# A mixture-of-experts stage with weights stationary, in blocks of 240 gathered tokens instead of tiles of 128

## The reference

```python
x = x + xattn(layernorm(x), ctx, ctx, ...)
x = x + ffn(layernorm(x), ...)
...
probs = softmax(xf @ router_w.T); topk_p, topk_i = top_k(probs, 2)
topk_p = topk_p / topk_p.sum(-1)
for e in range(8):
    mask = (topk_i == e).any(-1); w_tok = (topk_p * (topk_i == e)).sum(-1)
    mean_w = w_tok.sum() / mask.sum()
    h = silu(xf @ gate_w[e].T) * (xf @ up_w[e].T)          # 256 -> 1024
    out += mask[:, None] * (h @ down_w[e].T) * mean_w      # 1024 -> 256
```

## Time and profile before

| | |
|---|---|
| device time, median of 3 runs | 531.59 us (530.47 to 532.20) |
| profiled execution: span from first to last instruction | 528.9 us |
| instructions | 10721 |
| PE matmul busy | 476.4 us (90%) |
| PE weight loads busy | 375.3 us (71%) |
| DVE busy | 321.5 us (61%) |
| ACT busy | 265.6 us (50%) |
| POOL busy | 186.4 us (35%) |
| mean granted TensorE clock | 0.954 of full speed |
| DMA traffic | 46.26 MB, mean 87 GB/s |

### The profile page before, as it was taken

The page is one execution under the profiler, slowest core; times in us unless marked ns, Lnnn a source line. Parts: engine busy times, 40 slices in busy tenths (PEclk is TensorE's granted clock), DMA queues, the critical chain, the costliest instruction groups (busy, mean ns, idle before and its releaser), DMA issues. The chain is left out here.

```text
span 528.9 us, 10721 instructions
## 1 busy us (share of the span) xinstructions
PE 476.4 (90%) x2879; PEld 375.3 (71%) x2880; DVE 321.5 (61%) x827; ACT 265.6 (50%) x878; POOL 186.4 (35%) x211
## 2 busy tenths in 40 slices
PE   2999999999999983199999999999999999999980
PEld 2656666665666542078888888888888888888870
DVE  3476988989998656345665456655655555553430
ACT  1287777677777870044544445544444444532320
POOL 5201327355372434712332323323333232232232
PEclk9699999999999995579999999999999999999996
DMA  7166102112020171371531634415317212112110
GB/s 210 33 184 241 32 12 54 32 34 63 7 58 14 50 286 47 96 274 32 168 117 35 215 83 139 147 32 196 101 20 256 42 20 32 27 21 39 20 20 10
DMA packets 21738, 46.26 MB, mean 87 GB/s; under 512 B 5032, under 2 KB 18600, under 8 KB 20684
## 3 DMA queue, kind: packets, MB, share of 16 engines
q10 hardware_dynamic: 1982, 23.29, 11.6%
q1 hardware_dynamic: 12974, 14.34, 9.3%
q0 software_dynamic: 6752, 8.29, 9.2%
HBM read 34.21 MB, written 10.04 MB: 84 GB/s over the span
## 5 line engine op out<-in xcount | busy, mean ns | idle before, releaser
L752 ACT ACTIVATE probs<-b_s,negmax 100x100 f32<-100x100 f32 x256 | 85.6, 358 | 25.2 <-DVE negmax L1005 21.8
L615 PE MATMUL b_s<-w_hi,x_hi 128*128 128x512 f32 x180 | 77.1, 428 | 1.1 <-issue 1.1
L617 PE MATMUL b_s<-w_hi,x_lo 128*128 128x512 f32 x180 | 72.3, 402 | 0.0
L616 PE MATMUL b_s<-w_lo,x_hi 128*128 128x512 f32 x180 | 72.2, 401 | 0.0
L640 PE MATMUL b_pv<-w_hi,h_hi 128*128 128x256 f32 x240 | 69.8, 291 | 1.4 <-DVE h_lo L1102 1.4
L640 PE MATMUL b_pv<-w_hi,h_lo 128*128 128x256 f32 x240 | 67.4, 281 | 0.0
L640 PE MATMUL b_pv<-w_lo,h_hi 128*128 128x256 f32 x240 | 67.3, 280 | 0.0
L1245 POOL TENSOR_SCALAR y_sb<-y_raw,mean 128x256 f32<-128x256 f32 x30 | 32.8, 1093 | 75.9 <-DVE y_raw L1109 75.7
L1250 POOL DMA_INDIRECT out<-y_sb,idnow x30 | 49.1, 1638 | 25.6 <-issue 23.0
L780 ACT CAST h_hi<-b_small 128x512 fp32r<-128x512 f32 x30 | 17.6, 587 | 80.7 <-PE b_small L631 80.7
L1116 DVE TENSOR_TENSOR w_lo<-w_raw,w_hi x84 | 57.3, 682 | 0.0
(11 more groups left out here) (142 smaller groups left out, 1004.1 us busy)
## 6 DMA issues: line engine op xcount, KB each, us to landing
w_raw<-in_ffw ACTq DMA_DIRECT2D x7, 3072.0 KB, 10.1
xin<-slots SPq DMA_DIRECT2D x30, 128.5 KB
w_raw<-in_ffw SPq DMA_DIRECT2D x1, 3072.0 KB, 10.8
kblk<-krot SPq DMA_DIRECT2D x128, 12.5 KB, 1.8
out<-x_all SPq DMA_DIRECT2D x8, 200.0 KB
ctx_all<-in_ctxT SPq DMA_DIRECT2D x1, 1200.0 KB, 6.1
x_all<-in_x SPq DMA_DIRECT2D x1, 1200.0 KB
cst<-in_consts SPq DMA_DIRECT2D x1, 539.0 KB, 7.5
```

The costliest lines, as they stand in the source:

```text
L615: pe.matmul(o, lh, rh, start=(k == 0), stop=False)
L616: pe.matmul(o, lh, rl, start=False, stop=False)
L617: m = pe.matmul(o, ll, rh, start=False, stop=(k == n - 1))
L752: m = nc.scalar.activation(probs[:, N % 3, h, :], b_s[N % 3][0:S, h * S:(h + 1) * S], ACT.Exp, bias=negmax[:, N % 4, h:h + 1], accum_out=p ...
```

## The change

The expert stage is rewritten. A block is 240 gathered tokens, in two groups of 120 rows (`GRP`, `ROWS`, `TILE`). In gate and up the weights are now the stationary operand and the block's 240 tokens the moving one, so the result comes out as features x tokens, for one chunk `f` of 128 hidden features at a time (eight chunks, `FC`). It is already in the form that the down projection needs, and `hidden_transpose` is gone. The down projection runs per chunk and group: 3 matmuls with 120 stationary and 256 moving columns, for 2 groups.

ACT makes `h_hi` of a chunk from `h_sb` in SBUF (which DVE's `gated` has written), not from a transposed PSUM bank. The weights of the next expert are split in six pieces of 1024 columns (`WC`, `WCH`), one after each of the first six chunks of the expert's first block. There is one `w_raw` buffer in place of two; each piece is loaded again (`reload`, on ACT's queue) once its low part is made. The scale by the mean weight is done by ACT's `take_output`, straight from PSUM; POOL only copies row numbers and issues two indirect DMAs per block. The tails are gone: SP fills `slots` with padding rows by DRAM to DRAM DMAs during the attention stage (`fill_pads`, 8 for each of the first seven pairs), and POOL's scatter waits for those that cover its rows. SP reads the loop's two values ahead of the wait for the scatters. ACT's loop over experts is written out. The plan word loses its third field.

```diff
-TILE = 128
+GRP = 2
+ROWS = 120
+TILE = GRP * ROWS
...
-WC = 512
-CH = WT // WC
-WCH = THIRDS * CH
+WC = WT // 2
+WCH = 6
...
@@ sync
+            def fill_pads(j):
+                for e in range(E):
+                    base = e * REGION + j * TILE
+                    sp.dma_start(slots[base:base + TILE, :].rearrange("(p g) w -> p (g w)", g=GRP),
+                                 padrows.rearrange("(p g) w -> p (g w)", g=GRP)).then_inc(s_pre[j], 16)
...
                     key_blocks(i + 1)
+                if i < MAXT:
+                    fill_pads(i)
...
-                sp.wait_ge(s_tails[e], 16)
...
@@ tensor
+            def hidden(par, f):
+                cols = slice(f * P, (f + 1) * P)
+                for which, banks, done in ((0, b_gate, s_gate), (1, b_up, s_up)):
+                    wh, wl = wpart(w_hi[par])[which], wpart(w_lo[par])[which]
+                    o = banks[f % 2][:, 0:TILE]
+                    for c in range(DC):
+                        pe.matmul(o, wh[:, c, cols], x_hi[:, c, :], start=(c == 0), stop=False)
+                        pe.matmul(o, wh[:, c, cols], x_lo[:, c, :], start=False, stop=False)
+                        m = pe.matmul(o, wl[:, c, cols], x_hi[:, c, :], start=False, stop=(c == DC - 1))
+                    m.then_inc(done, 1)
+            def project_down(par, t, f):
+                pe.wait_ge(s_hlo, FC * t + f + 1)
+                if f == 0:
+                    pe.wait_ge(s_y, t + 1)
...
+                for g in range(GRP):
+                    o = b_y[g // 2][0:ROWS, g % 2 * D:(g % 2 + 1) * D]
+                    for k, (left, right) in enumerate(((h_hi, wh), (h_hi, wl), (h_lo, wh))):
+                        m = pe.matmul(o, left[:, f, g * ROWS:(g + 1) * ROWS], right[:, f, :], ...)
+            def step(t, par, next_par, next_split, following):
+                for f in range(1, FC):
+                    if f >= 2:
+                        pe.wait_ge(s_h, FC * t + f - 1)
+                    if f == FC - 1:
...
+                            pe.wait_ge(s_xlo, t + 1)
+                            tile_transpose(t + 1)
+                    hidden(par, f)
+                    if f >= 2:
+                        project_down(par, t, f - 2)
+                project_down(par, t, FC - 2)
...
                     pe.wait_ge(s_wlo, next_split)
                     pe.wait_ge(s_xlo, t + 2)
                     hidden(next_par, 0)
+                project_down(par, t, FC - 1)
@@ scalar
+            def hidden_high(t, f):
+                a.wait_ge(s_h, FC * t + f + 1)
+                nc.scalar.copy(h_hi[:, f, :], h_sb[:, f % 2, :]).then_inc(s_hhi, 1)
+            def weights_high(e, par, k):
+                a.wait_ge(s_raw[k], 16 * (e + 1))
+                cols = slice(k * WC, (k + 1) * WC)
+                nc.scalar.copy(w_hi[1 - par][:, cols], w_raw[:, cols]).then_inc(s_whi, 1)
+            def reload(e, k):
+                a.wait_ge(s_wlo, WCH * (e + 1) + k + 1)
+                a.dma_start(w_raw[:, k * WC:(k + 1) * WC],
+                            ffw[e + 2][:, k * WC:(k + 1) * WC]).then_inc(s_raw[k], 16)
+            def take_output(t, e):
+                a.wait_ge(s_down, t + 1)
+                a.wait_ge(s_idnow, t + 1)
...
+                    m = nc.scalar.activation(y_sb[:, 2 * n:2 * n + 2, :].rearrange("p g d -> p (g d)"),
+                                             b_y[n][0:ROWS, :], ACT.Copy, scale=meanw[0:ROWS, e:e + 1])
+            def step(t, e, par, split, again, final=False):
+                for f in range(FC):
+                    if f:
+                        if f == FC - 1 and not final:
+                            a.wait_ge(s_up, FC * (t + 1))
+                            x_high(t + 1)
+                        silu(t, f)
+                    hidden_high(t, f)
+                    if split and f < WCH:
+                        weights_high(e, par, f)
+                    if split and again and 1 <= f <= WCH:
+                        reload(e, f - 1)
                 if not final:
                     silu(t + 1, 0)
+                take_output(t, e)
@@ vector
+            def gated(t, f):
+                v.wait_ge(s_up, FC * t + f + 1)
+                v.wait_ge(s_act, FC * t + f + 1)
+                V.tensor_tensor(h_sb[:, f % 2, :], b_up[f % 2][:, 0:TILE], act[:, f % 2, :], ALU.mult).then_inc(s_h, 1)
+            def hidden_low(t, f):
+                v.wait_ge(s_hhi, FC * t + f + 1)
+                V.tensor_tensor(h_lo[:, f, :], h_sb[:, f % 2, :], h_hi[:, f, :], ALU.subtract).then_inc(s_hlo, 1)
+            def weights_low(e, par, k):
+                v.wait_ge(s_whi, WCH * e + k + 1)
+                cols = slice(k * WC, (k + 1) * WC)
+                V.tensor_tensor(w_lo[1 - par][:, cols], w_raw[:, cols], w_hi[1 - par][:, cols],
+                                ALU.subtract).then_inc(s_wlo, 1)
+            def step(t, e, par, split, final=False):
+                for f in range(FC):
+                    if f:
+                        if f == FC - 1 and not final:
+                            x_low(t + 1)
+                        gated(t, f)
+                    hidden_low(t, f)
+                    if split and f < WCH:
+                        weights_low(e, par, f)
+                    if f == FC - 2 and not final:
+                        v.wait_ge(s_idnow, t + 1)
+                        take_ids(t + 1)
                 if not final:
                     gated(t + 1, 0)
+            def expert(e, par):
+                lo, hi, end, _ = tiles_of(v, e)
+                step(lo, e, par, True)
+                with v.If(end - lo), v.Fori(lo + 1, hi) as t:
+                    step(t, e, par, False)
@@ gpsimd
-            for e in range(E):
-                G.indirect_dma_start(slots, bass.IndirectOffsetOnAxis(taili[:, e:e + 1], 0),
-                                     tailrow[:, :], None).then_inc(s_tails[e], 16)
...
+                for n in range(GRP):
+                    G.indirect_dma_start(out, bass.IndirectOffsetOnAxis(idnow[:, n:n + 1], 0), y_sb[:, n, :], None,
...
+                                         compute_op=ALU.add).then_inc(s_add, 16)
```

More of the change, by code:

```diff
@@ L642, in project_down @@
-                m.then_inc(s_down, 1)
-            def step(t, par, split_down, next_par, next_split, following):
-                hidden_transpose(t, 0)
-                hidden(par, 1)
-                with ExitStack() as s:
-                    if following is not None:
-                        s.enter_context(pe.If(following))
-                    tile_transpose(t + 1)
-                pe.wait_ge(s_wlo, split_down)
-                pe.wait_ge(s_y, t + 1)
-                project_down(par, t, 0)
-                hidden_transpose(t, 1)
+                        m = pe.matmul(o, left[:, f, g * ROWS:(g + 1) * ROWS], right[:, f, :],
+                                      start=(f == 0 and k == 0 and g % 2 == 0), stop=(f == FC - 1 and k == 2),
+                                      skip_group_check=True)
@@ L783, in weights_high @@
-            def weights_high(par, third, chunk):
-                if third is None:
-                    return
-                col = third * WT + chunk * WC
-                nc.scalar.copy(w_hi[1 - par][:, bass.ds(col, WC)], w_raw[par][:, bass.ds(col, WC)]).then_inc(s_whi, 1)
-            def step(t, third, par, final=False):
-                hidden_high(t, 0)
-                weights_high(par, third, 0)
-                silu(t, 1)
-                weights_high(par, third, 1)
-                if not final:
-                    x_high(t + 1)
-                weights_high(par, third, 2)
-                hidden_high(t, 1)
-                weights_high(par, third, 3)
+                for c in range(DC):
+                    m = nc.scalar.copy(x_hi[:, c, :], b_xt[c][:, 0:TILE])
@@ L1086, in x_low, with take_ids @@
                 v.wait_ge(s_xhi, t + 1)
-                V.tensor_tensor(x_lo[:, :, :].rearrange("p c t -> p (c t)"), b_xt[:, 0:DC * TILE],
-                                x_hi[:, :, :].rearrange("p c t -> p (c t)"), ALU.subtract).then_inc(s_xlo, 1)
-            def take_ids(t, column):
+                for c in range(DC):
+                    ins = V.tensor_tensor(x_lo[:, c, :], b_xt[c][:, 0:TILE], x_hi[:, c, :], ALU.subtract)
+                ins.then_inc(s_xlo, 1)
+            def take_ids(t):
@@ L1134, in step @@
                 if not final:
                     gated(t + 1, 0)
-            def expert(e, par, split):
-                lo, hi, end, m, _ = tiles_of(v, e)
-                if not split:
-                    with v.If(end - lo), v.Fori(lo, end) as t:
-                        step(e, t, None, par)
-                    step(e, end, None, par, final=True)
-                    take_output(hi)
-                    return
-                left = v.snap((THIRDS - (m - lo)) & 3)
-                with v.If(left), v.Fori(0, left) as third:
-                    for n in range(CH):
```

(7 more changed lines are left out.)

311 lines of the change are left out of this document (110 added, 201 removed).

## The result

| | before | after |
|---|---|---|
| device time, median of 4 runs | 531.04 us (530.47 to 532.20) | 565.26 us (564.74 to 565.84) |
| ratio, 95% interval | | 1.064 (1.062 to 1.066) |
| span of the profiled execution | 528.9 us | 564.0 us |
| PE matmul busy | 476.4 us (90%) | 476.2 us (84%) |
| DVE, ACT busy | 61%, 50% | 59%, 51% |

The changed kernel is 34 us slower. The forecast was 549.4, 18 us slower, with a range to 570: the right side, with the right mechanism in the expert stage, but about half of the size, and 7.5 us came by a mechanism that it did not have. The busy time on PE is the same as before; the difference is waiting.

The account below looks back on a forecast made before the run. TensorE's order was taken to pace the expert stage, with the ring pacing first blocks after the change; 528.9 + 18.8 (stage) - 2 (start) + 1.0 (end) + 2.7 (profiled span to median) = 549.4 us, range 511 to 570.

Parts of the forecast that it names:

- the ring: Expert's first block: weights_high, weights_low, gated, hidden_high wait in a circle across ACT and DVE, 2.94 us per chunk.
- B: Expert stage: the ring is hidden and PE sets the pace, 513.5 us in total; chance 0.09.
- C: PE's matmuls: the fast rate doesn't hold below 256 columns, 0.405 us for 240, 966 us in total; chance 0.14.
- D: Split blocks: PE's waits drop its clock to 0.5, a block takes 33 us, 626 in total; chance 0.03.
- E: PE: narrower matmuls no longer cover the weight loads, a step takes 2.96 us, 630 in total; chance 0.03.
- F: The ring holds, and fills delay each key-block transfer by about a microsecond or the start gains nothing: 557 us; chance 0.04.
- I take **0** (ends -1 and +8): Attention stage: the added padding DMAs fit in the gap between key-block transfers, costing 0 us, from -1 to +8.
- the stage: Expert stage, first tile transpose to last output copy: 312.5 us for 293.7 before, +18.8.
- A second block: An expert's second block, without weight splitting: PE sets the pace, 16.9 us, seven times.
- a first block with a split: First block of an expert, splitting the next weights: 22.2 us, six times after the stage's first block of 28.6.
- the last expert's two: Last expert's two blocks: 16.9 + 15.5 (no next block) = 32.4 us.
- Around the stage: Start -2 us (ends -3 and 0) from the removed tails and earlier loop values; end +1.0 us for the output.

Follow-up runs that it names:

- a_ring: Changed kernel with DVE's subtraction of weight piece f-1 moved behind gated(f) and ACT's reloads one chunk later: 534.54 us.
- a_fillfew: Changed kernel with padding rows written only for the first two blocks of each expert's region, 16 DMAs instead of 56: 565.05 us.
- a_pool512: Changed kernel with POOL splitting the first expert's weights in pieces of 512 columns again, not 1024: 557.81 us.
- b_pool1024: Kernel before with POOL's two pieces of 512 columns put together in one of 1024: 538.88 us, ratio 1.013.
- a_plan2: a_best with PE reading the plan words of two experts at once, at the head of its loop over pairs of experts: 526.35 us.
- a_hoist: a_best with POOL's pieces of 256 columns, PE's expert loop written out, the next plan word read ahead of each expert's last block: 519.13 us.
- a_best: Changed kernel with POOL's 512-column pieces, DVE's weight piece f-1 behind gated(f), and silu(f) ahead of weights_high(f-1) on ACT: 526.26 us, ratio 0.991.
- b_pool256: Kernel before with POOL's pieces of the first expert's weights 256 columns wide, not 512: 530.34 us, ratio 0.999.

## Why the forecast was half the size

**Right, with the size:** the 240-column matmul (0.113 for 0.111), the chunk on PE (2.06 for 2.04), the ring (2.96 for 2.94) and what releases whom in it, the unchanged number of padded rows, the clock (0.50 at the stage's start, from 224 to 234 us, as the sum took it, and 1.00 from 254 to 540), the padding DMAs on SP (5.0 us, hidden). a_ring is the proof of the main step: order alone is worth 30.7 us. Not right was where PE waits for the ring: for h_sb ahead of the next hidden (0.64 us), not for h_lo ahead of each down product. This changes no term of the sum, since the ring sets the time of a turn either way. Of the rivals B, C, D and E none came true; C fell with the first 240-column row. F's sign did show, a stage that begins later than before, but not its cause: a_fillfew takes most of the fills away and gains nothing.

**The step that failed** is "I take **0** (ends -1 and +8)" for the attention stage. It asked only what the new DMAs would do there. It overlooked that the same edit of WC widens POOL's pieces there too, from 512 to 1024 columns, and doesn't name them; POOL's work in all is the same, and only the length of one instruction grows. The runs put 7.5 us on that (a_pool512, b_pool1024), and none on the DMAs (a_fillfew). Of the 9.0 us between the two traces 8.1 went with that edit (first transpose at 222.69 in a_pool512, 230.78 in the changed kernel); the other 0.9 is within what this start differs by between kernels with the same attention stage (1.9 us from a_ring to the changed kernel). The end of the range, +8, held the 7.5, by another cause than the one that it was given for; that the total lies within the range owes as much to luck.

**Mis-sized, the stage:** +27.2 us for +18.8. A second block is 17.28 for 16.9, seven times (2.7 us); a first block with a split 22.95 for 22.2, six times (4.5); and the last expert's two are 33.5 for 32.4 (1.1). In the second block 0.16 is the chunk (8 x 0.02), and 0.1 the end of the block, where PE stands still for 0.29 us ahead of the next hidden(0), not 0.2. A further 0.1 is that the matmul after such a stop comes 0.22 us ahead of its successor, not 0.11 (314.11 and 314.33). In the first block, counted as in the forecast from its first hidden_high (317.31), 0.1 is the ring's five turns, and 0.1 more is lost up to the end of x_lo (19.6 for 19.4); the next hidden(0) ends at 21.2 for 20.7, and take_output starts at 22.1 for 21.6. The last 0.24 lies between the start of take_output and the next hidden_high at an expert's boundary: 0.83 us, not 0.59 (316.48 to 317.31).

The last expert's first block is 18.17 for 16.9. There PE reads and unpacks the plan word, 0.7 to 0.8 us by a_plan2. The kernel before does this as well, and at its seven boundaries between experts PE has no such wait; its only one, 1.1 us, is at the stage's start (224.71). Probably the twelve down products behind its last wait covered it, where six are left now; that was not tried apart from a_hoist. The forecast priced no instruction of the sequencers (register loads and their unpacking, branches, loops) at all. In the changed kernel the ring hides this at six boundaries: PE's issue waits are 0.6 and 1.0 us there as in a_best, yet the first blocks with the longer wait are no longer than the others (22.93, 22.93, 22.70 against 22.95, 23.21, 22.94), as they are in a_best (18.6 against 18.1). So only the last expert pays; in a_best all seven do.

**Around the stage:** xin left 2.4 us after the last scatter's end, against 5.0 before: 2.6 gained, the forecast said 2.2. But from that issue to the first transpose it is 3.1 us for 1.7, where 0.3 more was forecast, so the start gained 1.2 and not 2. Whether this is the bytes is open: with the small tile it was 1.7, 2.4 and 4.1 us in the kernel before, b_pool256 and b_pool1024, with the large one 2.9 to 3.3 in every kernel. From the start of the last output copy to the end of the span it is 12.7 before and 13.0 after, 0.3 longer, where 1.0 was forecast; counted from that copy's end, as the stage is, both have 12.3.

So the sum: 9.0 (attention) - 1.2 (start) + 27.2 (stage) + 0.0 = 35.0, for a difference of the spans of 35.1.

## What to carry to other kernels

When work is put between the steps of a chain that goes back and forth between two engines, draw the ring: if each engine's next link stands behind its filler, the fillers of both add up, though each engine is busy for little more than half of the time. Put the filler behind the link that the other engine waits for, and the same work is nearly free (30.7 of 565 us here). When a tile size changes, look for every other place that uses the constant: a GpSimd instruction twice as long on the same total work can hold VectorE in a stage that nobody meant to touch.

## What the runs showed that was not expected

- DVE's xn write ends about 0.15 us after POOL's running subtraction, at each of the three widths: mean 678 ns at 256 columns, 1056 at 512, 1810 to 1839 at 1024. The work that POOL does in all is the same.
- Reading and unpacking one plan word costs PE's sequencer 0.7 to 0.8 us, and a turn of the loop around it 0.4. The kernel before has both and no wait for them at its boundaries; here they show as "issue", 0.6 and 1.0 us.
- An ACT activation with a per-row scale from PSUM, 120 x 512, takes 687 ns, where a plain copy of 128 x 512 takes 587.
- The rate of the rounded type holds below 256 columns: 0.113 us for 240, against 0.118 for 256. The 128-column weight loads have records of 190 ns each, one for every matmul, and the matmuls still start every 0.113 us.
